# Eight step sums in four PSUM banks instead of four, and one-hots ten steps ahead

## The chip, the cores and the metric

The kernel runs on one core of a Trainium2 chip, as one launch. The metric is the device time of that core in microseconds, the median of the runs shown; lower is better. TensorE is PE in the profile (its weight loads PEld), VectorE is DVE, ScalarE is ACT, GpSimd is POOL and SyncE is SP.

## The reference, cut to what matters

One layer of a graph transformer over 6250 nodes of 256 features and 100,000 edges: two graph convolutions, linear attention beside them, then a mixture of eight experts with the best two for each node. The change touches the sum over edges in the two convolutions:

```python
xw = x @ W
msg = xw[src] * norm[:, None]
out = jax.ops.segment_sum(msg, dst, num_segments=num_nodes)
return out + b
```

`dst` is sorted. `src` is random, so that the rows of the table have to be gathered one edge at a time.

## The kernel before

Everything is fp32. After a preparation of some 100 us the kernel runs the sum of layer 0 (with the keys, values and queries of the attention woven in), a dense part, the sum of layer 1 (with the rest of the attention woven in), then the routing, then the experts. The order is written out by hand: every engine has its own unrolled program, and semaphores tie them.

**The sum.** The 782 tiles of 128 edges and the 49 blocks of 128 nodes give 833 steps (STEPS). A step is one pair of tile and block. Four engines work on it in a chain:

- POOL (`gathers`, L628) fetches one tile at a time, 128 rows of 1 KB, by an indirect DMA into one of 32 places (ROWS). Before it uses a place again it waits for a count `freed` that SP gives.
- SP (`tiles_here`) waits for each tile's transfer and then counts up `here` (L644). For the tile 16 behind it (BEHIND) it waits until the tensor engine's count `summed` has reached the first step of the next tile, and then counts up `freed` (L650). It does both for one tile after the other, in order.
- PE (`step_sum`, L689) multiplies a one-hot matrix, 128 edges by 128 nodes, with the tile: one fp32 matmul of 128x128 by 128x256, which the trace shows as two LDWEIGHTS and two MATMUL records. It writes 256 words of a PSUM bank, half of it, and counts up `summed`. It waits for `here`, and for `added` to reach s - 3: there are four banks (PSB), so step s needs the one of step s - 4 read.
- DVE (`step_add`, L679) waits for `summed` to reach s + 1 and adds the bank's half onto `acc` in SBUF, at an address from a register, and counts up `added`. Every fourth step it also makes the one-hots of four steps (`four_selects`, L657), six steps ahead (AHEAD) in twelve places (SELS), and reads four registers for the next addresses.

**Woven in.** Sixteen steps make a turn, one for each block of nodes. After its step k of a turn an engine does other work (`between`). In layer 0, PE has two transposes at k = 0 (L805), the q, k, v product at k = 3 (L814), for which it waits until ACT has copied the transposes, and the context product at k = 13 (L821, L823), for which it waits for DVE's keys. DVE has three operations at k = 8 (L771, L774, L778), for which it waits for ACT's exponential (L757). In layer 1, DVE makes `qd` at k = 5 (L1043, L1045, L1049) and PE transposes it at k = 8 (L1090), with a wait for it; at k = 11 PE waits for ACT again.

Of the kernel before, what the change touches and what calls it, by code (L numbers as in the profile page):

```python
# [9 lines left out]
ALU = mybir.AluOpType  # L10
# [4 lines left out]
P = 128  # L15
N, D, E = 6250, 256, 100000
# [8 lines left out]
STEPS = NT * SPI  # L25
# [5 lines left out]
PAIRS = -(-NT // 2)  # L31
assert BLOCKS >= 2 * PAIRS + 2
SG = -(-STEPS // P)
ROWS, SELS, FOUR = 32, 12, 4
LOADED = 4
TURN = 16
BEHIND, FREED_AT = 16, 8
# [24 lines left out]
WEIGHTS_AT = 9  # L62
LN_EPS = 1e-5
DEN_MIN = 1e-6
AHEAD = 6
PSB = 4
assert AHEAD >= PSB + 2 and SELS == 3 * FOUR and STEPS <= SG * P - FOUR


def gps_layer(nc, x, src, dst, wqkv, wproj, bproj, gw1, gb1, gw2, gb2, wr, br, wide, vectors, out):  # L70
# [3 lines left out]
    def sem(name):  # L74
        if name not in sems:
            sems[name] = nc.alloc_semaphore(name=name)
        return sems[name]
# [12 lines left out]
    def sb(ctx, name, shape, dt=F32):  # L90
        return ctx.enter_context(nc.sbuf_tensor(name, shape, dt))
# [33 lines left out]
    with whole, nc.allow_non_contiguous_dma("a few columns of one word"):  # L125
# [524 lines left out]
                    sp.sem_inc(sem(f"freed{layer}"), 1)  # L650

        def step_bank(s):
            return step_ps[s % PSB][:, 0:D]

        def four_selects(v, layer, s):

            v.tensor_tensor(sel[:, s % SELS:s % SELS + FOUR, :], iota_n[:, None, :].to_broadcast([P, FOUR, P]),  # L657
                            dloc[:, s:s + FOUR, None].to_broadcast([P, FOUR, P]), ALU.is_equal
                            ).then_inc(sem(f"selected{layer}"), 1)

        def blocks_of(s):

            _, regs = nc.values_load_multi_w_load_instructions(
                words[1:2, s:min(s + LOADED, STEPS), 0], engines=(DVE_ENGINE,), min_val=0, max_val=(BLOCKS - 1) * D,
                skip_runtime_bounds_check_because="a step's tile is one of the step's number or less, by less than the blocks")
            return list(regs)
# [6 lines left out]
            return list(regs)  # L673

        def step_add(v, layer, s, block):
            if s > 0:
                v.wait_ge(sem(f"added{layer}"), s)
            to = acc[:, bass.ds(block, D)]
            v.tensor_tensor(to, to, step_bank(s), ALU.add).wait_op(sem(f"summed{layer}"), s + 1, "sem-ge"  # L679
                                                                   ).then_inc(sem(f"added{layer}"), 1)  # L680

        def step_sum(t, layer, s, here):
            slot = t.snap(here & (ROWS - 1))
            t.to_reg(slot)
            if s < PSB:
                t.wait_ge(sem(f"selected{layer}"), s // FOUR + 1)
            else:
                t.wait_ge(sem(f"added{layer}"), s - PSB + 1)
            t.matmul(step_bank(s), sel[:, s % SELS, :], rows_flat[:, bass.ds(slot * D, D)], start=True, stop=True  # L689
                     ).wait_op(sem(f"here{layer}"), t.to_reg(here), "sem-ge").then_inc(sem(f"summed{layer}"), 1)  # L690

        def vector_steps(v, layer, between):

            blocks = blocks_of(0)
            for s in range(0, 2 * FOUR, FOUR):
                four_selects(v, layer, s)
            for s in range(STEPS):
                if s % LOADED == 1 and s + LOADED - 1 < STEPS:
                    blocks.extend(blocks_of(s + LOADED - 1))
                if s % FOUR == 2 and s + AHEAD < STEPS:  # L700
                    four_selects(v, layer, s + AHEAD)
                step_add(v, layer, s, blocks[s])
                if s < NT * TURN:
                    between(s // TURN, s % TURN)

        def tensor_steps(t, layer, between):

            tiles = tiles_of(0)
            for s in range(STEPS):
                step_sum(t, layer, s, tiles[s])  # L710
                if s % LOADED == 1 and s + LOADED - 1 < STEPS:
                    tiles.extend(tiles_of(s + LOADED - 1))
                if s < NT * TURN:
                    between(s // TURN, s % TURN)
# [8 lines left out]
        with ExitStack() as ph:  # L723
# [10 lines left out]
            step_ps, ps_t, ps_q, ps_v, ps_c, ps_k = bk[0:PSB], bk[PSB], bk[PSB + 1], bk[PSB + 2], bk[PSB + 3], bk[PSB + 3][:, D:]  # L734
# [230 lines left out]
        with ExitStack() as ph:  # L965
# [14 lines left out]
            step_ps, ps_t, ps_d, ps_t2, ps_o = bk[0:PSB], bk[PSB], bk[PSB + 1], bk[PSB + 2], bk[PSB + 3]  # L980
            with nc.Block() as block:
# [53 lines left out]
                def _(v):  # L1035
                    def between(i, k):
# [20 lines left out]
                        if k == TURN - 2:  # L1057
# [5 lines left out]
                            v.wait_ge(sem("a_mix"), i + 1)  # L1063
                            v.tensor_tensor(tile(node, i), tile(node, i), mixb[:, :], ALU.add).then_inc(sem("a_node"), 1)
                    vector_steps(v, 1, between)

                @block.tensor
# [36 lines left out]
        with ExitStack() as ph:  # L1104
# [43 lines left out]
            ge = sb(ph, "ge", [1, FT, NX])  # L1148
# [514 lines left out]
```

## Time and profile before

| | |
|---|---|
| median of 3 runs | 3344.09 us (3339.18 to 3347.60) |
| the profiled execution | 3348.99 us, its span 3346.7 us |
| granted TensorE clock, mean | 0.817 |
| PE, DVE, ACT, POOL busy | 72%, 52%, 19%, 60% of the span |
| sum of layer 0, first to last gather | 100.39 to 1238.40 us of the span |
| sum of layer 1, first to last gather | 1337.10 to 2470.40 us |

Times of instructions count from the start of the span. "Idle before" is the time that an engine did nothing before an instruction, with the one that ended the wait: "SPq L650" is SP's count `freed`, "SPq L644" its count `here`; "issue" and "remote" name no instruction of another engine.

### The profile page before, as it was taken

How to read it: one execution, taken by the hardware profiler on the slowest of the kernel's cores; microseconds unless marked ns; L12 is line 12 of the kernel's file. 1: busy time of each engine (PE TensorE's matmuls, PEld its weight loads, DVE VectorE, ACT ScalarE, POOL GpSimd, SP SyncE). 2: the span in 40 equal slices, each digit the busy share in tenths (PEclk: the TensorE clock that was granted, in tenths of full speed). 3: DMA queues.
4: the chain of work that ended last, by engine and by line, in shares of the span. 5: the costliest groups of instructions: out<-in, count | busy, mean ns of one | idle time of the engine just before them, and what ended most of it. 6: DMA issues, size and time to landing. Idle time of an engine off the chain costs nothing. (4 is left out here: it accounts for less than half of the span.)

```text
span 3346.7 us, 47049 instructions
## 1 busy us (share of the span) xinstructions
PE 2393.5 (72%) x11743; PEld 1816.8 (54%) x11743; DVE 1734.3 (52%) x4351; ACT 620.0 (19%) x1318; POOL 1994.5 (60%) x2107
## 2 busy tenths in 40 slices
PE   3376676666777768366666666666769399999998
PEld 2144444444444446244344444444448199999998
DVE  6144444444444456244444445554556766666665
ACT  1000000000000005000001010101116344444443
POOL 1576766666666653766666666666743055555554
PEclk9777888888777789666767778777779599999999
DMA  6433332333333322444444444444422455555551
GB/s 150 131 94 90 91 92 87 90 91 90 88 90 92 88 77 82 120 137 143 144 137 146 146 136 146 146 147 146 146 73 77 158 180 147 146 147 149 147 147 20
DMA packets 178034, 397.68 MB, mean 119 GB/s; under 512 B 42398, under 2 KB 96575, under 8 KB 169644
## 3 DMA queue, kind: packets, MB, share of 16 engines
q0 software_dynamic: 96800, 233.29, 26.1%
q1 hardware_dynamic: 46516, 99.22, 8.2%
q10 hardware_dynamic: 34552, 63.24, 5.8%
q8 instruction: 69, 1.13, 0.1%
q14 instruction: 97, 0.79, 0.1%
HBM read 323.27 MB, written 75.01 MB: 119 GB/s over the span
## 5 line engine op out<-in xcount | busy, mean ns | idle before, releaser
L628 POOL DMA_INDIRECT rows<-rows_layer,srcs x1564 | 1550.8, 992 | 751.8 <-issue 394.3
L689 PE MATMUL l_bank<-rows,sel 128*128 x3332 | 1207.3, 493 | 639.7 <-issue 246.1
L679 DVE TENSOR_TENSOR acc<-acc,l_bank 128x256 f32 x1666 | 699.5, 420 | 1234.9 <-remote 493.7
L689 PEld LDWEIGHTS l_bank<-rows,sel 128*128 128x128 f32 x3332 | 710.2, 238 | 1012.3 <-issue 468.8
L657 DVE TENSOR_TENSOR sel<-iota_n,dloc 128x512 f32<-128x512 f32 x418 | 286.5, 686 | 20.1 <-issue 20.1
L1574 POOL DMA_INDIRECT out<-ys,g_sum x112 | 180.9, 1615 | 190.0 <-DVE ys L1530 164.8
L1491 ACT ACTIVATE hr<-ffn_bank,vec 128x256 f32<-128x256 f32 x448 | 213.0, 475 | 385.4 <-PE ffn_bank L1432 362.0
L1430 PE MATMUL ffn_bank<-wh,hhi 128*128 128x256 f32 x896 | 257.6, 288 | 0.0
L1430 PE MATMUL ffn_bank<-xh,wh 128*128 128x256 f32 x896 | 252.3, 282 | 2.4 <-DVE xl L1506 2.4
L1432 PE MATMUL ffn_bank<-wh,hlo 128*128 128x256 f32 x896 | 253.1, 282 | 0.0
L1432 PE MATMUL ffn_bank<-xh,wl 128*128 128x256 f32 x896 | 251.9, 281 | 0.0
L1431 PE MATMUL ffn_bank<-xl,wh 128*128 128x256 f32 x896 | 251.9, 281 | 0.0
L1431 PE MATMUL ffn_bank<-wl,hhi 128*128 128x256 f32 x896 | 251.3, 281 | 0.0
L814 PE MATMUL l_bank<-w_qkv,xt 128*128 128x512 f32 (+1 forms) x392 | 179.4, 611 | 42.5 <-issue 28.5
L1515 DVE TENSOR_TENSOR hlo<-hr,hhi 128x256 fp32r<-128x256 f32 x448 | 191.3, 427 | 15.4
L1430 PEld LDWEIGHTS ffn_bank<-xh,wh 128*128 128x128 f32 x896 | 169.8, 189 | 2.8 <-DVE xl L1506 2.8
L1545 POOL DMA_INDIRECT xr<-rows_x,g_row x112 | 133.4, 1191 | 63.3 <-POOL g_row L1541 44.5
L1431 PEld LDWEIGHTS ffn_bank<-wl,hhi 128*128 128x128 f32 x896 | 170.4, 190 | 0.0
L1431 PEld LDWEIGHTS ffn_bank<-xl,wh 128*128 128x128 f32 x896 | 169.9, 190 | 0.0
L1432 PEld LDWEIGHTS ffn_bank<-xh,wl 128*128 128x128 f32 x896 | 169.7, 189 | 0.0
L1430 PEld LDWEIGHTS ffn_bank<-wh,hhi 128*128 128x128 f32 x896 | 168.3, 188 | 0.0
L1432 PEld LDWEIGHTS ffn_bank<-wh,hlo 128*128 128x128 f32 x896 | 167.7, 187 | 0.0
(274 smaller groups left out, 2319.6 us busy)
## 6 DMA issues: line engine op xcount, KB each, us to landing
wh<-w_hi SPq DMA_DIRECT2D x32, 1024.0 KB
wl<-w_lo SPq DMA_DIRECT2D x32, 1024.0 KB
rows<-rows_layer,srcs POOLq DMA_INDIRECT x1564
w_qkv<-wide ACTq DMA_DIRECT2D x49, 335.0 KB
w_hi<-whi ACTq DMA_DIRECT2D x49, 335.0 KB
w_lo<-wlo ACTq DMA_DIRECT2D x49, 335.0 KB
rows_layer<-acc SPq DMA_DIRECT2D x25, 256.0 KB, 2.1
rows_x<-acc SPq DMA_DIRECT2D x7, 910.0 KB
```

The source lines that it names most:

```text
L628: pool.indirect_dma_start(rows[:, (n + 1) % ROWS, :], None, table[layer], bass.IndirectOffsetOnAxis(ap=srcs[:, n:n + 1], axis=0)).then_inc ...
L657: v.tensor_tensor(sel[:, s % SELS:s % SELS + FOUR, :], iota_n[:, None, :].to_broadcast([P, FOUR, P]), dloc[:, s:s + FOUR, None].to_broadca ...
L679: v.tensor_tensor(to, to, step_bank(s), ALU.add).wait_op(sem(f"summed{layer}"), s + 1, "sem-ge").then_inc(sem(f"added{layer}"), 1)
L689: t.matmul(step_bank(s), sel[:, s % SELS, :], rows_flat[:, bass.ds(slot * D, D)], start=True, stop=True).wait_op(sem(f"here{layer}"), t.to ...
L814: ins = t.matmul(to[:, 0:n], xt[:, c, :], w_qkv[:, c, lo:lo + n], start=(c == 0), stop=(c == KC - 1))
L1430: t.matmul(to, a[0], b[0], start=first, stop=False)
L1431: t.matmul(to, a[0], b[1], start=False, stop=False)
L1432: return t.matmul(to, a[1], b[0], start=False, stop=last)
L1491: a.activation(hr[:, m % 4, :], ps_h[m % 4][:, 0:TS], ACT.Gelu, bias=vec[q][:, O_B1 + m:O_B1 + m + 1]).then_inc(sem("e_g"), 1)
L1515: v.tensor_tensor(hl[q][:, m, :], hr[:, m % 4, :], hh[q][:, m, :].bitcast(F32), ALU.subtract).then_inc(sem("e_hs"), 1)
L1545: pool.indirect_dma_start(xr[q][:, h, :], None, rows_x, bass.IndirectOffsetOnAxis(ap=g_row[q][:, h:h + 1], axis=0)).then_inc(sem(f"rows_{q ...
L1574: pool.indirect_dma_start(out, bass.IndirectOffsetOnAxis(ap=g_sum[q][:, h:h + 1], axis=0), ys[q][:, h, :], None, bounds_check=N - 1, oob_i ...
```

## The change

Two following steps share a bank: the even step takes its first 256 words, the odd step the second. With four banks PE may have eight sums written and not yet added. PE waits only ahead of an even step, until both sums of the bank have been added (those of steps s - 8 and s - 7). DVE waits, at the even step, until both sums of the bank are written, then adds one and the other; the odd step waits only for the add before it. The one-hots are made ten steps ahead, in sixteen places, with three groups of four before the first step instead of two.

```diff
--- before.py
+++ after.py
@@ -31,7 +31,7 @@
 PAIRS = -(-NT // 2)
 assert BLOCKS >= 2 * PAIRS + 2
 SG = -(-STEPS // P)
-ROWS, SELS, FOUR = 32, 12, 4
+ROWS, SELS, FOUR = 32, 16, 4
 LOADED = 4
 TURN = 16
 BEHIND, FREED_AT = 16, 8
@@ -62,9 +62,10 @@
 WEIGHTS_AT = 9
 LN_EPS = 1e-5
 DEN_MIN = 1e-6
-AHEAD = 6
 PSB = 4
-assert AHEAD >= PSB + 2 and SELS == 3 * FOUR and STEPS <= SG * P - FOUR
+SUMS = 2 * PSB
+AHEAD = SUMS + 2
+assert AHEAD % FOUR == 2 and SELS >= AHEAD + FOUR + 2 and SELS % FOUR == 0 and STEPS <= SG * P - FOUR
 
 
 def gps_layer(nc, x, src, dst, wqkv, wproj, bproj, gw1, gb1, gw2, gb2, wr, br, wide, vectors, out):
@@ -650,7 +651,7 @@
                     sp.sem_inc(sem(f"freed{layer}"), 1)
 
         def step_bank(s):
-            return step_ps[s % PSB][:, 0:D]
+            return step_ps[s // 2 % PSB][:, s % 2 * D:(s % 2 + 1) * D]
 
         def four_selects(v, layer, s):
 
@@ -673,26 +674,30 @@
             return list(regs)
 
         def step_add(v, layer, s, block):
-            if s > 0:
-                v.wait_ge(sem(f"added{layer}"), s)
             to = acc[:, bass.ds(block, D)]
-            v.tensor_tensor(to, to, step_bank(s), ALU.add).wait_op(sem(f"summed{layer}"), s + 1, "sem-ge"
-                                                                   ).then_inc(sem(f"added{layer}"), 1)
+            if s % 2 == 0:
+                if s > 0:
+                    v.wait_ge(sem(f"added{layer}"), s)
+                v.tensor_tensor(to, to, step_bank(s), ALU.add).wait_op(
+                    sem(f"summed{layer}"), min(s + 2, STEPS), "sem-ge").then_inc(sem(f"added{layer}"), 1)
+            else:
+                v.tensor_tensor(to, to, step_bank(s), ALU.add).wait_op(
+                    sem(f"added{layer}"), s, "sem-ge").then_inc(sem(f"added{layer}"), 1)
 
         def step_sum(t, layer, s, here):
             slot = t.snap(here & (ROWS - 1))
             t.to_reg(slot)
-            if s < PSB:
+            if s < SUMS:
                 t.wait_ge(sem(f"selected{layer}"), s // FOUR + 1)
-            else:
-                t.wait_ge(sem(f"added{layer}"), s - PSB + 1)
+            elif s % 2 == 0:
+                t.wait_ge(sem(f"added{layer}"), s - SUMS + 2)
             t.matmul(step_bank(s), sel[:, s % SELS, :], rows_flat[:, bass.ds(slot * D, D)], start=True, stop=True
                      ).wait_op(sem(f"here{layer}"), t.to_reg(here), "sem-ge").then_inc(sem(f"summed{layer}"), 1)
 
         def vector_steps(v, layer, between):
 
             blocks = blocks_of(0)
-            for s in range(0, 2 * FOUR, FOUR):
+            for s in range(0, AHEAD + 2, FOUR):
                 four_selects(v, layer, s)
             for s in range(STEPS):
                 if s % LOADED == 1 and s + LOADED - 1 < STEPS:
```

## Rows read from the trace of the kernel before

**Rows 1.** The page's costliest groups: the four of the sums.

```profile
L628 POOL DMA_INDIRECT rows<-rows_layer,srcs x1564 | 1550.8, 992 | 751.8 <-issue 394.3
L689 PE MATMUL l_bank<-rows,sel 128*128 x3332 | 1207.3, 493 | 639.7 <-issue 246.1
L679 DVE TENSOR_TENSOR acc<-acc,l_bank 128x256 f32 x1666 | 699.5, 420 | 1234.9 <-remote 493.7
...
L657 DVE TENSOR_TENSOR sel<-iota_n,dloc 128x512 f32<-128x512 f32 x418 | 286.5, 686 | 20.1 <-issue 20.1
```

**Rows 2.** Layer sums and their ends: PE, PEld, DVE, ACT, POOL busy us (count), clock, DMA.

```profile
100.39:1238.40 1138.01, 771.41 (x2486) 484.08 (x2484) 497.77 (x1144) 86.15 (x196) 778.95 (x782) 0.80 0.31 91
1238.40:1267.80 29.40, 21.80 (x70) 13.79 (x70) 19.67 (x46) 0.00 (x0) 0.02 (x1) 0.86 0.02 6
1337.10:2470.40 1133.30, 719.30 (x2192) 477.68 (x2192) 549.85 (x1296) 106.99 (x244) 771.47 (x782) 0.72 0.47 141
2470.40:2497.40 27.00, 18.92 (x62) 11.01 (x62) 17.92 (x41) 0.00 (x0) 0.36 (x1) 0.94 0.02 5
```

**Rows 3.** Who waited for whom, whole span: us in total, times, longest.

```profile
DVE acc L679 <- remote: 493.7, 172, 16.5
...
DVE acc L679 <- PE l_bank L689: 455.5, 366, 4.5
...
POOL rows L628 <- SPq L650: 323.3, 330, 6.9
...
PE l_bank L689 <- DVE acc L679: 165.3, 128, 16.3
```

**Rows 4.** Timeline 594 to 614 us, layer 0: one slow stretch and its end.

```profile
594.17 2.74 PE L814 MATMUL l_bank<-w_qkv,xt 128*128 128x512 f32 x8
...
596.75 1.89 PE L689 MATMUL l_bank<-rows,sel 128*128 x8
...
602.48 0.60 ACT L757 ACTIVATE eq<-l_bank 128x512 f32<-128x512 f32 x1 [9.46 <-remote]
...
603.90 0.42 DVE L679 TENSOR_TENSOR acc<-acc,l_bank 128x256 f32 x1 [7.46 <-issue]
...
604.46 1.22 PE L689 MATMUL l_bank<-rows,sel 128*128 x2 [5.82 <-issue]
606.01 0.42 DVE L679 TENSOR_TENSOR acc<-acc,l_bank 128x256 f32 x1 [1.69 <-PE l_bank L689]
606.28 0.95 POOL L628 DMA_INDIRECT rows<-rows_layer,srcs  x1 [2.33 <-SPq L650]
...
609.95 0.42 DVE L679 TENSOR_TENSOR acc<-acc,l_bank 128x256 f32 x1 [0.35 <-PE l_bank L689]
...
610.29 0.69 DVE L657 TENSOR_TENSOR sel<-iota_n,dloc 128x512 f32<-128x512 f32 x1
...
610.89 1.52 DVE L679 TENSOR_TENSOR acc<-acc,l_bank 128x256 f32 x3
...
613.11 0.42 DVE L679 TENSOR_TENSOR acc<-acc,l_bank 128x256 f32 x1 [0.70 <-DVE acc L679]
```

**Rows 5.** Timeline 145 to 168 us: the end of the first long run of gathers.

```profile
148.06 1.21 PE L689 MATMUL l_bank<-rows,sel 128*128 x2 [4.65 <-issue]
...
157.41 0.96 POOL L628 DMA_INDIRECT rows<-rows_layer,srcs  x1 [0.30 <-issue]
165.01 1.52 DVE L679 TENSOR_TENSOR acc<-acc,l_bank 128x256 f32 x3 [16.49 <-remote]
...
165.28 0.95 POOL L628 DMA_INDIRECT rows<-rows_layer,srcs  x1 [6.92 <-SPq L650]
```

**Rows 6.** Timeline 95 to 106 us: the start of layer 0's sum.

```profile
100.79 1.30 DVE L657 TENSOR_TENSOR sel<-iota_n,dloc 128x512 f32<-128x512 f32 x2 [15.36 <-issue]
...
103.16 1.22 PE L689 MATMUL l_bank<-rows,sel 128*128 x2 [1.97 <-SPq L644]
```

**Rows 7.** Line L1049 (`qd`, layer 1): who waited for it, us and times.

```profile
  PEld l_bank L1090: 20.3, 20
```

## The prediction

> **What bounds the kernel now.** I read the page's groups first, then the busy time of the two stretches that hold the sums, then the waits, and last the timeline of a few single stretches. The groups [rows 1] say where the time can be: the four instructions of a step are the costliest of the kernel, and POOL, PE and DVE each have hundreds of microseconds of idle time in front of them. The stretches [rows 2] say that the gathers span 1138 and 1133 us of the 3347, with 782 gathers in each, one per 1.45 us. No engine is full there: POOL 68%, PE 68 and 63%, DVE 44 and 49%. The change can act only here and in the 29 and 27 us that follow the last gather; the rest does not contain a line of it.
>
> POOL has the highest floor. When it isn't held, it issues a gather every 0.96 + 0.30 = 1.26 us [rows 5]; 781 intervals of that are 984 us. What lies above is 1138.0 - 779.0 - 781 x 0.30 = 124.8 us of pauses in layer 0 and 1133.3 - 771.5 - 234.3 = 127.5 us in layer 1, 252 us in all, and a little for gathers that take longer than 0.96 us (the mean is 0.99). The waits [rows 3] name the cause of the pauses: POOL waits for SP's `freed`. So POOL has filled its 32 places and waits until a tile 31 or so behind has been summed. The sums are late, not the gathers.
>
> Why they are late is the point on which all hangs. DVE waits 456 us for PE by name and 494 us for something that the profile can't name [rows 3]; PE's wait for DVE, that is for a free bank, is only 165 us. The timeline [rows 4] shows such a wait from near. The q, k, v product and four steps of PE are on record from 594.17 to 598.64 us. ACT, which waits for the first, starts at 602.48, and DVE, which waits for the first of the four steps, at 603.90, after 7.46 us idle. PE has used up its four places meanwhile and stands until 604.46, just behind that add. All the time POOL issues a gather each 1.26 us, until its places are full; then it pauses for 2.33 us, in which DVE gets its second sum at 606.01, and SP lets POOL go on at 606.28. The first run of gathers shows the same, larger [rows 5]: PE's step at 148.06 is followed by nothing, POOL issues its last gather at 157.41, and at 165.01 three adds run without a gap. Finished sums arrive slowly while POOL issues without a pause, and in a bunch when it has stopped. What carries this inside the chip the trace doesn't tell. In this kernel POOL stops only when its ring is full.
>
> **The change, part by part.**
>
> More sums ahead. With eight places PE can have eight steps on the way in a slow stretch instead of four, so that up to four more sums arrive in the bunch at its end and SP can free up to four tiles more before POOL's ring is full again. I cost it by pauses. If all are like the one at 606.28, 2.33 - 0.30 = 2.03 us above the usual gap [rows 4], 252 us are 124 pauses, one for 1564 / 124 = 12.6 gathers or 1666 / 124 = 13.4 steps. Four more steps for each would make 17.4 and cut the pauses to 0.77, by 58 us. But PE can't run ahead freely: its own waits in the turn stop it, in layer 0 at k = 3 for ACT and at k = 13 for DVE's step 8, in layer 1 at k = 8 for DVE's step 5, which allows a lead of three, less than four banks already give, and at k = 11 for ACT. I take two thirds of the effect in layer 0 and one third in layer 1, half in all: 29 us. The bounds are nothing (the bunch is no larger, or POOL fills its ring again in the same time) and the whole 252 us.
>
> How the rows of PE are read weighs here. ACT starts 5.6 us behind the recorded end of the product that it waits for [rows 4], so a record of PE can end before its result counts. By its records, though, PE is idle before L689 for want of DVE's add for 165.3 us [rows 3]; taken at their word these go with the deeper ring, and the time would be 3349 - 165 = 3184 us. The Trainium skill's page Perfetto Trace Analysis, section Tensor Engine Instruction (MATMUL, LD_WEIGHTS), says that the end of a matmul is computed from its size and not observed, so that a PE row doesn't prove that the sum is there. The trace agrees, by those 5.6 us. I go by them, and not by PE's idle time: its wait for a bank is then mostly a wait for sums that are late themselves, and more banks don't bring those sooner; that reading is the sum of 29 us above.
>
> The end of each layer. After the last gather 29.4 and 27.0 us pass with no POOL at all; DVE is busy for 19.7 and 17.9 of them [rows 2]. Its own pace, four steps with one group of one-hots, is 613.11 - 609.95 = 3.16 us (the add at 609.95, the group at 610.29, three adds from 610.89, the next at 613.11 [rows 4]), 0.79 us for a step. A deeper ring lets it keep nearer to this: I take 5 us for each layer, 10 in all, between nothing and the idle 9.7 + 9.1 = 19 us.
>
> The waits of DVE and PE. The number of matmuls, adds and counts is unchanged. DVE keeps its two waits for a pair of steps on the sums as one, and odd steps no longer hold the sequencer for `added`. The gap between adds that follow without a stall is (1.52 - 3 x 0.42) / 2 = 0.13 us [rows 4]; if the odd step lost all of it, 833 x 0.13 = 108 us of DVE time would go. DVE is busy less than half of these stretches, so the idle time of [rows 3] hides this; I count nothing on the path, with 108 us as its far bound were DVE the limit, and nothing as the near one.
>
> The cost of pairs. The even add now waits for the odd sum as well. That is the price of the shared bank, and it holds up what stands behind it on DVE: the one-hots, the three operations at k = 8 in layer 0, and `qd` at k = 5 in layer 1. The one-hots are made ten steps ahead, and PE is at most eight ahead: nothing. The others are the rival below; for the likeliest case I count nothing, since PE reaches its wait for the keys five steps later.
>
> The one-hots. As many groups as before, 418 of 0.69 us [rows 1]; four more places cost only SBUF. A third group ahead of the first step moves 0.69 us before the first add of each layer. The first two end at 102.09, PE starts at 103.16 on the first tile and takes 1.22 us on record [rows 6], so the first add can't start before 104.38. The third ends near 102.8: hidden. Without that cover it would cost 1.4 us for both layers.
>
> **The sum.** -29 - 10 = -39 us on the profiled execution's 3349.0: 3310. The median of the runs stands 4.9 us below that execution, so 3305 us, 1.2% faster. A change of 0.3%, 10 us, is about the least that a measurement of this kernel tells from none.
>
> **The rivals.**
>
> *No gain.* Sums reach DVE and SP at the pace that POOL's gathers leave them, however many are on the way. For it: in the first long run PE's step at 148.06 stood on record for 17 us before the adds of 165.01 [rows 5], and POOL's cycle of run and pause could close again at the same 1.45 us. Against it: the bunch at the end of a stall is as long as the ring. Time: 3344, within 10 us. It decides if the pauses are needed to clear the way: then their sum stays at 252 us.
>
> *A large gain.* POOL is never held. For it: PE and DVE are 32 to 56% idle, so nothing but the coupling keeps them. Against it: the waits in the turns, and the slow stretches themselves. With all pauses gone 3344 - 252 - 10 = 3082; by PE's own records 3344 - 165 = 3179. I give weight only to its nearer part, gains over 4%.
>
> *Slower, by the pairs.* In layer 0 the keys at k = 8 stand behind the add of step 8, which now also waits for step 9. Sums late in a slow stretch follow each other by 606.01 - 603.90 = 2.11 us [rows 4], and PE's products at k = 13 wait for the keys. In layer 1 `qd` is behind the add of step 5, and the add of step 4, formerly done by then, now comes with it: 0.55 us (0.42 and the gap of 0.13) in front of `qd`, for which PE waits at k = 8 already now, 20 times with 20.3 us [rows 7]. 49 turns each: at most 49 x 2.11 = 103 us and 49 x 0.55 = 27 us. The loss passes to the end only where PE's wait delays `freed`; at a third of both, 43 us, it outweighs the 39 us of gain, and from there the change is slower. Should the gain be missing as well, half of both gives 3344 + 65 = 3409; one third, the likelier, 3387. The Trainium skill's page PSUM — Partial Sum Buffer, section PSUM bank collisions raise a hardware error, forbids two engines in one bank at a time, even in different columns, so that a kernel can't drop this wait of the pair; no run here shows such a collision.
>
> **How the numbers follow.** Gain by more sums ahead, 0.3 to 4%: 0.46. Gain over 4%: 0.12. No change within 0.3%: 0.22. Slower through the pairs: 0.20. Faster is thus 0.58, same 0.22, slower 0.20. The range goes from 3190 us, a little beyond 4% into the large gain (up to PE's 165 us), to 3375 us, three quarters of the one-third case of the slower rival; about 0.17 is left outside. The likeliest case alone is 3215 to 3333.
>
> **What would show it.** Right: POOL's idle time before L628 falls from 751.8 by some 30 us and the waits for SPq L650 become fewer; the stretches after the last gathers fall to about 24 and 22 us; DVE's L679 shows rows of more adds in a bunch. No gain: the same pause sum, the same 1.45 us for a gather, though PE's waits for DVE's add are gone. Slower: more idle time before L821 in layer 0 and L1090 in layer 1, and more of POOL's time on SPq L650. The prediction is wrong above all if the late sums come from something that the deeper ring itself feeds or relieves: then the pauses move by far more than four steps' worth, either way.

## The result, and the profile after

The changed kernel takes 3335.05 us (median of 5, 3329.50 to 3340.59), the kernel before, beside it, 3344.93 us (median of 5, 3339.18 to 3351.41): a ratio of 0.9964, 95% interval 0.9952 to 0.9976. It is 0.36% faster, 9.9 us, where 39 us were forecast. The profiled execution took 3340.59 us, 8.4 us less than the one of before; its span is 3338.3 us.

The same two kernels were later timed again in two further groups of runs: 0.9959 (0.9945 to 0.9973) and 0.9975 (0.9964 to 0.9986). The gain is small, but it is there.

The page's groups of the changed kernel, with the lines shifted by one to five (the gathers are L629 now, the steps of PE L694, the even and the odd add L681 and L684):

```profile
L629 POOL DMA_INDIRECT rows<-rows_layer,srcs x1564 | 1553.0, 993 | 742.6 <-issue 395.3
L694 PE MATMUL l_bank<-rows,sel 128*128 x3332 | 1040.8, 459 | 215.8 <-DVE acc L684 93.4
...
L681 DVE TENSOR_TENSOR acc<-acc,l_bank 128x256 f32 x834 | 349.1, 419 | 932.9 <-remote 582.6
L684 DVE TENSOR_TENSOR acc<-acc,l_bank 128x256 f32 x832 | 349.9, 421 | 287.6 <-issue 169.5
L819 PE MATMUL l_bank<-w_qkv,xt 128*128 128x512 f32 (+1 forms) x392 | 204.6, 683 | 216.0 <-issue 195.5
L658 DVE TENSOR_TENSOR sel<-iota_n,dloc 128x512 f32<-128x512 f32 x418 | 288.5, 691 | 20.0 <-issue 20.0
```

Against [rows 1], PE's idle time before its steps is a third of what it was, 215.8 us for 639.7, and that of POOL before its gathers has hardly moved, 742.6 for 751.8. DVE's idle time before its adds is 932.9 + 287.6 = 1220.5 us for 1234.9.

The busy time of the two stretches of gathers and of what follows each of them (columns as in [rows 2]):

```profile
104.63:1236.39 1131.76, 705.05 (x2502) 503.90 (x2500) 502.59 (x1150) 86.17 (x196) 775.66 (x782) 0.78 0.32 91
1236.39:1260.93 24.54, 16.13 (x56) 10.33 (x54) 16.98 (x40) 0.00 (x0) 0.01 (x1) 0.93 0.03 6
1331.02:2463.92 1132.90, 683.39 (x2204) 487.69 (x2204) 550.15 (x1298) 107.63 (x244) 777.31 (x782) 0.73 0.47 141
2463.92:2489.47 25.55, 15.87 (x51) 10.37 (x50) 16.97 (x39) 0.00 (x0) 0.00 (x0) 0.87 0.02 6
```

Worked out as in the prediction, POOL's pauses (its idle time above the usual 0.30 us behind each gather) are 1131.76 - 775.66 - 234.3 = 121.8 and 1132.90 - 777.31 - 234.3 = 121.3 us, 243 in all, where they were 252. The ends took 24.54 + 25.55 = 50.1 us, where they took 56.4. So this pair of traces has 9.2 us less in pauses, of which gathers that took longer use up 2.6, and 6.3 us less at the ends. The changed kernel's first gather came 4.2 us later than the other's, which gives part of it back; that leaves the 8.4 us between the spans. The waits:

```profile
DVE acc L681 <- remote: 582.6, 135, 20.8
...
POOL rows L629 <- SPq L651: 314.3, 308, 6.8
...
DVE acc L681 <- PE l_bank L694: 256.2, 129, 9.6
...
PE l_bank L694 <- DVE acc L684: 93.4, 68, 7.3
```

PE waits less for DVE, 93.4 us for 165.3 [rows 3], and POOL waits for SP's `freed` as it did, 314.3 us for 323.3. The rows with `<-remote`, 582.6 us here and 493.7 before, can be named: by the trace's own list of semaphore updates, each of these waits ended at a count of `summed` that is on record more than 1.5 us after the end that PE's last step has on record. They are waits for PE's sums, late ones. The list has gaps: of the 833 counts of `summed` in a layer it holds about 690 and 638 before, 668 and 604 after. So some late sums stand under "issue" too.

The end of the first long run of gathers shows why:

```profile
151.77 0.42 DVE L681 TENSOR_TENSOR acc<-acc,l_bank 128x256 f32 x1 [10.32 <-issue]
...
161.79 0.95 POOL L629 DMA_INDIRECT rows<-rows_layer,srcs  x1 [0.30 <-issue]
169.32 0.42 DVE L681 TENSOR_TENSOR acc<-acc,l_bank 128x256 f32 x1 [15.44 <-remote]
169.41 0.38 ACT L757 ACTIVATE xt<-l_bank 128x256 f32<-128x256 f32 x1 [51.95 <-remote]
169.55 0.95 POOL L629 DMA_INDIRECT rows<-rows_layer,srcs  x1 [6.81 <-SPq L651]
...
169.85 5.49 PE L819 MATMUL l_bank<-w_qkv,xt 128*128 128x512 f32 x8 [26.20 <-issue]
```

POOL pauses here for 6.81 us, as it did for 6.92 [rows 5], and the adds had stood for 15.44 us, as for 16.49. But PE had gone on past its steps and now stands for 26.20 us before the q, k, v product: it waits for ACT, and ACT waits for the transposes, which were late like everything else of PE's. That is where PE's idle time went. Of its products in the turns the kernel before shows

```profile
L814 PE MATMUL l_bank<-w_qkv,xt 128*128 128x512 f32 (+1 forms) x392 | 179.4, 611 | 42.5 <-issue 28.5 <-ACT xt L752 14.0
L821 PE MATMUL l_bank<-qk,vv 128*128 128x128 f32 x196 | 49.3, 341 | 17.8 <-issue 17.6
L1083 PE MATMUL l_bank<-ks_h,qt 128*128 128x8 f32 x196 | 38.9, 308 | 51.1 <-issue 28.8 <-ACT qt L1014 22.3
...
L1090 PE MATMUL l_bank<-ident,w_qkv 128*128 128x128 f32 x98 | 25.6, 352 | 21.2 <-issue 11.6 <-DVE w_qkv L1049 9.5
...
L1076 PE MATMUL l_bank<-ident,qc 128*128 128x128 f32 x98 | 22.7, 321 | 0.0
```

and the changed kernel, beside its L819 above:

```profile
L826 PE MATMUL l_bank<-qk,vv 128*128 128x128 f32 x196 | 56.5, 381 | 78.4 <-issue 41.9 <-DVE qk L783 36.5
L1088 PE MATMUL l_bank<-ks_h,qt 128*128 128x8 f32 x196 | 42.2, 325 | 125.5 <-ACT qt L1019 65.5 <-issue 60.0
...
L1095 PE MATMUL l_bank<-ident,w_qkv 128*128 128x128 f32 x98 | 26.2, 358 | 52.1 <-issue 26.7 <-DVE w_qkv L1054 25.3
L1081 PE MATMUL l_bank<-ident,qc 128*128 128x128 f32 x98 | 25.1, 348 | 141.9 <-ACT qc L1012 92.4 <-issue 49.5
```

The idle time before these five products was 42.5 + 17.8 + 51.1 + 21.2 + 0.0 = 132.6 us and is 216.0 + 78.4 + 125.5 + 52.1 + 141.9 = 613.9 us. With that before the steps it was 772 us and is 830: nothing of PE's waiting went away, it moved from the steps to the products. In the same way the sums grew older as PE got ahead. By the records of the trace, the median time (half of the steps lie below it) from the start of a step's first matmul to the start of its add was 3.1 and 2.8 us in the two layers and is 6.2 and 4.1 us.

The bunches can be counted as well, from the recorded updates of `summed` that follow each other within 0.1 us. Before, the largest bunch is four, the number of sums on the way, and there are 33 and 32 of these in the two layers. In the changed kernel 38 bunches of layer 0 have five to eight counts and 23 of layer 1 have five to eight, and the counts that come alone fell from 511 and 439 to 368 and 379. POOL's pauses did not become much fewer with it: gaps of more than 0.6 us between gathers went from 85 and 97 to 82 and 75, and the remaining ones are longer.

### The profile page after: what moved, and what is told of

Read it like the earlier page. It is cut to its first block and busy times, and to the rows that moved or that the text cites. A ratio compares the mean times of both kernels' runs of the same rounds, so it can differ in the third digit from the quotient of the medians.

```text
span 3338.3 us, 47049 instructions
## 1 busy us (share of the span) xinstructions
PE 2282.6 (68%) x11743; PEld 1842.1 (55%) x11743; DVE 1735.5 (52%) x4351; ACT 620.5 (19%) x1318; POOL 1995.7 (60%) x2107
## 5 line engine op out<-in xcount | busy, mean ns | idle before, releaser
L629 POOL DMA_INDIRECT rows<-rows_layer,srcs x1564 | 1553.0, 993 | 742.6 <-issue 395.3
L694 PE MATMUL l_bank<-rows,sel 128*128 x3332 | 1040.8, 459 | 215.8 <-DVE acc L684 93.4
L694 PEld LDWEIGHTS l_bank<-rows,sel 128*128 128x128 f32 x3332 | 730.6, 232 | 415.3 <-issue 185.9
L681 DVE TENSOR_TENSOR acc<-acc,l_bank 128x256 f32 x834 | 349.1, 419 | 932.9 <-remote 582.6
L684 DVE TENSOR_TENSOR acc<-acc,l_bank 128x256 f32 x832 | 349.9, 421 | 287.6 <-issue 169.5
L819 PE MATMUL l_bank<-w_qkv,xt 128*128 128x512 f32 (+1 forms) x392 | 204.6, 683 | 216.0 <-issue 195.5
L819 PEld LDWEIGHTS l_bank<-w_qkv,xt 128*128 128x128 f32 x392 | 99.8, 265 | 315.9 <-issue 287.9
```

The source lines that it names most:

```text
L629: pool.indirect_dma_start(rows[:, (n + 1) % ROWS, :], None, table[layer], bass.IndirectOffsetOnAxis(ap=srcs[:, n:n + 1], axis=0)).then_inc ...
L819: ins = t.matmul(to[:, 0:n], xt[:, c, :], w_qkv[:, c, lo:lo + n], start=(c == 0), stop=(c == KC - 1))
```

## The experiments

Eighteen kernels ran behind the first measurement, in six groups; those of a group shared the runs of the kernel before, and each ratio is taken within its group. The kernel before had two levels. It took 3344.93 us in the first measurement and 3346.28, 3365.71 and 3346.61 us in three groups, and 3051.74, 3046.46 and 3045.62 us in the other three. Each level held for every kernel and every run of its group. I first took it for a property of the chip, and some expectations below are worded so; the last group disproved it, since the chip with 3051.74 us took 3346.61 us there. What sets the level is not known. I call them the level of 3345 and the level of 3050. The change was designed, profiled and forecast at the level of 3345. The changed kernel was timed only there, in three measurements, and the kernels with two and three banks only at the other level, so that no run parts what the pairs do from what the depth does where sums are late.

**Pairs without more depth, and two kernels with the gathers set free.** This group met the level of 3050 (3051.74 us, 23 runs).

```diff
-PSB = 4
+PSB = 2
```

> Pairs without more depth: two banks hold four sums in pairs. Theory P (late sums come at the pace of the gathers, the number of places hardly matters): within 15 us of the changed kernel, at 3340 to 3355 us. Theory Q (depth is worth something and the pairs cost something that hides it): clearly slower than before, 3370 us or more, and the pair's price is the difference to before.

```diff
-PSB = 4
+PSB = 3
-AHEAD = SUMS + 2
+AHEAD = SUMS + 4
```

> Six sums in three banks. Theory P: within 6 us of the changed kernel (3335). Theory Q: between the two-bank kernel and the changed one, in proportion to the depth.

```diff
-            for n in range(ET):
-                if n >= ROWS:
-                    pool.wait_ge(sem(f"freed{layer}"), n - ROWS + 1)
-                pool.indirect_dma_start(rows[:, (n + 1) % ROWS, :], None, table[layer],
...
+            pool.memset(rows[:, :, :], 0.0).then_inc(sem(f"filled{layer}"), 1)
```

> Leaves out all 1564 gathers: the places are filled with zeros once per layer, SP counts the tiles without a transfer, everything else stays, so the output is not the reference's. Theory P (POOL's gathers make the sums late): no slow stretches; DVE's adds follow PE's records by 1 to 3 us, and each layer's sum takes 833 x 0.8 to 0.9 us plus the turns, 700 to 850 us instead of 1158. Theory R (the engines' own waits in the turns make them late): the layers stay above 1000 us and the slow stretches remain.

```diff
-                    sp.wait_ge(sem(f"summed{layer}"), until[m % FREED_AT])
...
-            t.matmul(step_bank(s), sel[:, s % SELS, :], rows_flat[:, bass.ds(slot * D, D)], start=True, stop=True
+            t.matmul(step_bank(s), sel[:, s % SELS, :], zero[:, :], start=True, stop=True
```

> The sums read a constant tile of zeros instead of the gathered rows, and SP frees a place as soon as the transfer 16 tiles on has landed, so that POOL is never held; the gathers and their number stay, the output is not the reference's. Theory P: POOL issues at 1.26 us all through, 985 us per layer, and as it never pauses the sums crawl all that time: many are still to do when the gathers end. Theory R: the layer ends shortly after the gathers, at 1010 to 1050 us, as the sums keep up.

Measured: two_banks 3057.37 us, 1.0023 (1.0014 to 1.0033); three_banks 3057.94 us, 1.0028 (1.0016 to 1.0039); free_gathers 3057.26 us; no_gathers 2441.26 us. At this level the sums of two_banks are never late: each of its 2 x 833 counts of `summed` is on record 0.013 to 0.015 us behind the recorded end of its step, and the list of updates has no gaps. Its two stretches of gathers:

```profile
100.90:1104.46 1003.56, 787.65 (x2542) 489.18 (x2540) 518.03 (x1183) 86.04 (x196) 765.48 (x782) 0.85 0.36 103
...
1181.40:2190.56 1009.16, 728.76 (x2244) 465.04 (x2244) 566.07 (x1330) 108.06 (x244) 771.21 (x782) 0.79 0.53 159
```

POOL's pauses are 1003.56 - 765.48 - 234.3 = 3.8 us and 3.7 us, where they were 125 and 128, and POOL is two to three gathers ahead of PE where it was 27. The pace is the floor of 1.26 us and a few hundredths. So depth can't be told from no depth here, and the forecasts of both theories for two_banks and three_banks (3335 us and above), which were made for the other level, stay untested. These three, and one_pass and before_half_ring of a later group, have five different edits and all lie 0.2 to 0.3% above the kernel before, free_gathers too, in which nothing of the sums holds POOL. I can't lay that to the pairs.

**The change again, with fewer counts, and with something behind each gather.** Level of 3345 (3346.28 us, 23 runs). The first two have no edit.

> The kernel before, for its profile on this chip. Theory C: with 3052 us no wait of DVE on 'remote' above 50 us in all, POOL's pauses below 50 us in all, 8 us from the last gather to the last add; with 3345 us the rows of the first profile.

> The changed kernel as it is, on the chip of this group. The first group ran where the kernel before took 3052 us instead of 3345, with POOL at its floor and no late sums. Theory C (the late sums belong to the circumstances of the first measurement, and where they are missing the change only costs): where the kernel before takes about 3052 us, this one is 0.2 to 0.4% slower, as the two- and three-bank kernels were; where it takes about 3345, 0.3 to 0.4% faster. Theory D (four pairs gain everywhere): faster in both.

```diff
-                     ).wait_op(sem(f"here{layer}"), t.to_reg(here), "sem-ge").then_inc(sem(f"summed{layer}"), 1)
+                           ).wait_op(sem(f"here{layer}"), t.to_reg(here), "sem-ge")
+            if s % 2 == 1:
+                ins.then_inc(sem(f"summed{layer}"), 2)
```

> The changed kernel with `summed` counted once per pair, up by two at the odd step. Theory P1 (late sums because each count of PE is slow to arrive): where the sums are late, half as many counts gives more than 1% over the changed kernel. Theory P2 (the path is held for a time, however many counts wait): same as the changed kernel within 0.3%. Where the sums aren't late: within 0.3% of the changed kernel, or slower by the half pair that SP waits longer.

```diff
+                pool.memset(idle[:, n:n + 1], 0.0)
```

> The changed kernel with one memset of one word per partition on POOL behind each gather, so that the gathers are issued at a slower and even pace. Theory P (the unbroken run of gathers makes the sums late): where the sums are late, they are late less, and the time falls although POOL does more. Where they aren't late: slower by 1564 times what the memset adds to POOL's interval, 100 to 250 us if that is 60 to 160 ns.

Measured: before_again 3344.16 us; after_again 3334.55 us, 0.9959 (0.9945 to 0.9973); one_count 3337.42 us, 0.9977 (0.9968 to 0.9987); paced 3343.61 us, 0.9997 (0.9986 to 1.0007). Stretches and ends of before_again and then of after_again:

```profile
104.32:1236.50 1132.18, 769.03 (x2482) 481.34 (x2480) 496.09 (x1142) 86.16 (x196) 775.03 (x782) 0.80 0.32 91
1236.50:1266.90 30.40, 23.25 (x76) 14.44 (x74) 20.54 (x48) 0.00 (x0) 0.01 (x1) 0.88 0.02 5
1335.79:2466.05 1130.26, 711.97 (x2192) 469.39 (x2192) 549.39 (x1295) 106.43 (x244) 768.13 (x782) 0.73 0.48 142
2466.05:2493.47 27.42, 19.09 (x63) 10.95 (x62) 18.33 (x42) 0.00 (x0) 0.00 (x0) 0.94 0.02 5
```

```profile
105.40:1237.42 1132.02, 712.32 (x2498) 504.13 (x2496) 501.89 (x1150) 86.02 (x196) 770.46 (x782) 0.78 0.32 91
1237.42:1261.64 24.22, 16.12 (x60) 9.84 (x58) 17.34 (x41) 0.00 (x0) 0.41 (x1) 0.97 0.02 7
1331.01:2462.52 1131.51, 666.00 (x2200) 478.83 (x2200) 549.79 (x1296) 107.61 (x244) 771.60 (x782) 0.74 0.48 141
2462.52:2489.26 26.74, 17.26 (x54) 11.42 (x54) 17.82 (x41) 0.00 (x0) 0.00 (x0) 0.87 0.02 6
```

The pauses are 250.7 and 252.9 us: the 9 us of the first pair of traces don't repeat, and can't be laid to the change. The ends are 57.8 and 51.0 us: the 6 us repeat. Some 3 to 5 us of the gain of 9 to 12 stay unplaced. Half as many counts by PE bring no time over the changed kernel (3337.42 us for 3334.55; its pauses are 237 us), so their number isn't what makes sums late. Paced didn't pace: POOL shows

```profile
593.32 0.96 POOL L630 DMA_INDIRECT rows<-rows_layer,srcs  x1 [0.19 <-issue]
594.27 0.12 POOL L633 MEMSET idle<- 128x1 f32 x1
594.58 0.96 POOL L630 DMA_INDIRECT rows<-rows_layer,srcs  x1 [0.19 <-issue]
```

A gather still comes each 1.26 us, the memset lies in the gap of 0.30 us. The kernel is 9 us slower than the changed kernel in the same group, and why is not known. It decides nothing on pacing.

**Real pacing, and rests.** This group met the level of 3050 (3046.46 us, 13 runs), where no sum is late. The edits of the first two are those of the kernels of their names; the others:

> The changed kernel without gathers, once more: its places are filled once with zeros and SP counts without a transfer; its output is not the reference's. It took 2441 us on the chip on which the kernel before took 3052 us, with sums of 698 and 709 us. Read only beside a kernel before of about 3345 us, where sums are late; at 3052 us it is a repetition. Theory 1 (sums are late because POOL issues gathers without a pause): 2441 us within 1%, no late sums, layers of about 700 us; all of the difference between the two chips is the gathers' doing. Rival (PE, DVE and SP signal late on that chip whatever POOL does): the late sums stay, and layers take over 850 us, 2750 us or more in all.

> The changed kernel with the same gathers, but the sums read a tile of zeros, and SP counts freed without waiting for summed, so that POOL is never held by a late sum; its output is not the reference's. On the chip with 3052 us it took 3057 us. Where the kernel before takes about 3345 us, theory 1 (unbroken gathers hold the sums back): POOL issues all 782 gathers at 1.26 to 1.29 us each, the sums fall ever further behind, DVE's last add comes 100 us or more after the last gather, and a layer is no shorter than before (1150 us), or hardly. Rival (POOL's waits for freed are the cost, and sums are late only within the lag that the ring allows): last adds within 35 us of the last gather, layers of 1040 us, and 3100 us in all.

```diff
+                pool.memset(idle[:, n % 2, :], 0.0).then_inc(sem(f"idle{layer}"), 1)
+                pool.wait_ge(sem(f"idle{layer}"), n + 1)
```

> The changed kernel, with a memset of 256 columns on POOL behind each gather (some 0.3 us) and a wait for it, so that gathers come every 1.40 to 1.45 us and never closer. Where the kernel before takes about 3345 us: theory 1 (what holds sums back is POOL issuing without a gap of some size): the sums come on time, the lag falls from 25 gathers to under 10, the tails from 25 to under 12 us, POOL's waits for freed go, and the time is 782 x 1.43 us for a layer, 3300 to 3330 us. Rival (what matters is the number of gathers on the way, or POOL must stand fully still): lag and waits as before, and the pace added: 3345 to 3400 us. Where the kernel before takes 3052 us both expect 782 x 2 x 0.15 = 235 us more, 3290 us.

```diff
+                if n % 8 == 7:
+                    pool.memset(idle[:, :], 0.0).then_inc(sem(f"idle{layer}"), 1)
+                    pool.wait_ge(sem(f"idle{layer}"), n // 8 + 1)
```

> The changed kernel, with one memset of 1600 columns on POOL behind each eighth gather (some 1.3 us) and a wait for it: POOL stands still with its gathers at a time of its own, before its ring is full. Where the kernel before takes about 3345 us: theory 1, with the pauses as what clears the way: late sums arrive in these pauses, the lag falls under 16, the tails under 15 us, and the pauses for freed (145 us for a layer in all) are replaced by 97 x 1.3 = 126 us: 3290 to 3335 us. Rival (a pause of 1.3 us is too short, sums need POOL's earlier gathers to drain): the waits for freed shrink by less than the rests add, 3340 to 3450 us. Where the kernel before takes 3052 us both expect about 2 x 110 us more, 3270 us.

Measured: no_gathers_2 2440.98 us; free_gathers_2 3051.04 us, 1.0018 (1.0008 to 1.0027); paced_wide 3516.61 us; rest_of_eight 3327.55 us. The last two show only that time added to POOL's gathers is time added to the kernel. The memset and its wait put 0.33 + 0.27 us behind each gather, 1.56 us from one to the next, more than I had reckoned (1.40 to 1.45), and the time grew by 470 us, not by 235. None of the four says anything on late sums. Whether pacing would help at the level of 3345 wasn't tried.

**Is it the gathers, and is it the ring.** Level of 3345 (3365.71 us, 17 runs). after_3 has no edit, no_gathers_3 the edit of no_gathers.

> The changed kernel itself. Where the kernel before takes about 3345 us: a repetition, 3335 us, ratio 0.996. Where it takes about 3050 us, no sum is late and PE never waits long for a bank, so that more depth buys nothing: theory 1 (the pairs delay the even add by one step and so `freed` and what stands behind it) gives a ratio of 1.002 to 1.003, as the kernels with two and three banks of pairs had there (1.0023 and 1.0028). Rival (depth makes up for the pairs): 0.998 to 1.000.

```diff
-ROWS, SELS, FOUR = 32, 16, 4
+ROWS, SELS, FOUR = 16, 16, 4
-BEHIND, FREED_AT = 16, 8
+BEHIND, FREED_AT = 8, 8
```

> The changed kernel with 16 places for gathered tiles instead of 32, and SP freeing the tile 8 behind instead of 16. Where the kernel before takes about 3345 us: theory 1 (POOL must stop for late sums to come, and it stops when its ring is full) says that POOL stops about as often again and each stop is shorter: lag near 12 instead of 25, tails 13 instead of 25 us, pace within 2% of 1.448 us, 3290 to 3350 us. Rival (what a stop costs is its own length, and there are twice as many): pace 1.6 us or more, 3550 us. Where the kernel before takes about 3050 us, the lag is 2 to 3 gathers and SP frees 8 behind: no change, 3055 to 3065 us.

> The changed kernel without gathers (places filled once with zeros, SP counts without a transfer; its output is not the reference's). It took 2441 us on both chips on which the kernel before takes 3050 us. Where the kernel before takes about 3345 us: theory 1 (late sums come from the gathers) 2441 us within 1% and no late sum; rival (PE, DVE and SP signal late there whatever POOL does) 2700 us or more.

Measured: after_3 3356.39 us, 0.9975 (0.9964 to 0.9986); half_ring 3326.07 us, 0.9886 (0.9869 to 0.9902); no_gathers_3 2441.57 us. Without gathers the level of 3345 is gone: the same 2441 us as at the other level. No wait is put down to "remote" before the adds any more. The adds of no_gathers_3:

```profile
L680 DVE TENSOR_TENSOR acc<-acc,l_bank 128x256 f32 x832 | 350.0, 421 | 253.6 <-DVE acc L677 211.9
L677 DVE TENSOR_TENSOR acc<-acc,l_bank 128x256 f32 x834 | 348.7, 418 | 85.0 <-PE l_bank L690 38.6
```

So sums are late only where gathers run (with the gathers their transfers are gone too, and the two weren't parted). The short ring tells more. Stretches and ends of after_3 and then of half_ring:

```profile
103.75:1242.63 1138.88, 719.62 (x2502) 511.76 (x2500) 503.58 (x1150) 86.02 (x196) 771.31 (x782) 0.78 0.31 91
1242.63:1268.05 25.42, 15.74 (x55) 10.38 (x54) 16.97 (x40) 0.00 (x0) 0.00 (x0) 0.93 0.03 7
1336.93:2477.06 1140.13, 672.16 (x2196) 477.46 (x2196) 548.47 (x1293) 107.86 (x244) 773.76 (x782) 0.74 0.48 140
2477.06:2505.94 28.88, 17.58 (x58) 11.10 (x58) 19.16 (x44) 0.00 (x0) 0.00 (x0) 0.85 0.02 5
```

```profile
100.07:1238.23 1138.16, 744.00 (x2527) 538.82 (x2525) 511.17 (x1168) 86.01 (x196) 774.02 (x782) 0.77 0.31 91
1238.23:1253.38 15.15, 10.23 (x30) 7.09 (x30) 9.46 (x23) 0.00 (x0) 0.00 (x1) 0.73 0.04 10
1323.20:2463.54 1140.34, 693.00 (x2234) 486.90 (x2235) 558.73 (x1319) 108.08 (x244) 771.37 (x782) 0.75 0.47 140
2463.54:2474.44 10.90, 5.84 (x21) 3.22 (x20) 7.86 (x18) 0.00 (x0) 0.00 (x0) 1.00 0.06 13
```

The gathers take the same 1138 and 1140 us with 32 places and with 16. The pauses are 265.4 and 264.5 us. And they are the same pauses: after_3's and then half_ring's wait for `freed` are

```profile
POOL rows L629 <- SPq L651: 320.8, 310, 6.8
```

```profile
POOL rows L629 <- SPq L651: 328.5, 306, 3.3
```

The longest is shorter, their number and sum are not. The rival had expected twice as many of the same length, a pace of 1.6 us or more. Theory 1 had the pace, the ends and the time. All of the gain lies at the ends: 54.3 us became 26.1, 28 us of the 30 by which half_ring beats after_3. POOL is some 26 tiles ahead of PE with 32 places and some 10 with 16, and what it is ahead by at its last gather has still to be summed.

**The short ring without the change, and one matmul record for a step.** The first pair met the level of 3050 (3045.62 us, 22 runs).

```diff
-ROWS, SELS, FOUR = 32, 12, 4
+ROWS, SELS, FOUR = 16, 12, 4
-BEHIND, FREED_AT = 16, 8
+BEHIND, FREED_AT = 8, 8
```

> The kernel before (four sums in four banks), with 16 places for gathered tiles instead of 32, and SP freeing the tile 8 behind. Where the kernel before takes 3345 to 3366 us: theory 1 (late sums come at a fixed rate while gathers run; only the tiles that POOL is ahead at the end cost time) gives the same 1.456 us per gather, tails of 13 to 16 us instead of 27 to 30, and 0.990 to 0.992 of the kernel before, so that the shorter ring gains three times what the change does. Rival (the short ring needs the eight sums on the way): 1.000 or more. Where the kernel before takes 3050 us, POOL is 2 to 3 gathers ahead: 0.999 to 1.001.

```diff
+            rows_high = rows_flat.bitcast(BF16).rearrange("p (n t) -> p t n", t=2)[:, 1, :]
-            sel = sb(ph, "sel0", [P, SELS, P])
+            sel = sb(ph, "sel0", [P, SELS, P], BF16)
-            t.matmul(step_bank(s), sel[:, s % SELS, :], rows_flat[:, bass.ds(slot * D, D)], start=True, stop=True
+            t.matmul(step_bank(s), sel[:, s % SELS, :], rows_high[:, bass.ds(slot * D, D)], start=True, stop=True
```

> The changed kernel with one-hots in bf16 and the tile read as the upper halves of its fp32 words, so that a step is one matmul record of PE instead of two; the gathered rows are cut to bf16 in the sums. Where the kernel before takes 3345 to 3366 us: theory 1 (while gathers run each matmul record of PE costs some 0.7 us until its result counts, two for a step, 1.4 us a step) halves the steps' share: sums keep up, the pace falls under 1.33 us per gather, and 3060 to 3170 us. Rival (the rate is per step, count or bank, not per record): 1.44 to 1.46 us per gather, 3300 to 3350 us. Where the kernel before takes 3050 us both expect 3040 to 3060 us, the gathers' own pace.

Measured: before_half_ring 3052.56 us, 1.0022 (1.0013 to 1.0031), a loss a little beyond what both sides allowed; one_pass 3053.13 us, 1.0026 (1.0016 to 1.0036). The last run has both edits on the kernel before, and met the level of 3345 (3346.61 us, 7 runs).

> The kernel before with 16 places instead of 32 (freed 8 behind), and with one-hots in bf16 and the tile read as the upper halves of its words, one matmul record a step; the gathered rows are cut to bf16 in the sums. Where the kernel before takes 3345 to 3366 us: theory 1 (0.7 us for each matmul record of PE while gathers run, two a step in the kernel before) brings the pace under 1.33 us per gather and the time to 3060 to 3170 us. Rival (the rate is not PE's records): 1.44 to 1.46 us per gather, and then the tails, 13 to 16 us with the short ring or 27 to 30 without its gain, say whether the short ring gains without the change: 3310 to 3330 us or 3340 to 3360 us. Where the kernel before takes 3050 us: 3045 to 3060 us by both.

Measured: 3297.17 us, 0.9860 (0.9841 to 0.9880), outside all three forecasts.

```profile
103.43:1232.65 1129.22, 542.74 (x1713) 294.46 (x1711) 511.27 (x1180) 86.02 (x196) 772.66 (x782) 0.62 0.32 91
1232.65:1238.68 6.03, 3.04 (x11) 1.72 (x10) 3.88 (x10) 0.00 (x0) 0.00 (x1) 0.50 0.08 24
1310.02:2434.23 1124.21, 442.88 (x1412) 218.05 (x1412) 558.45 (x1323) 107.17 (x244) 760.55 (x782) 0.52 0.48 142
2434.23:2442.75 8.52, 3.45 (x10) 0.94 (x9) 6.08 (x15) 0.00 (x0) 0.00 (x0) 0.50 0.06 16
```

With half of PE's records for the steps the pauses are 122.3 + 129.4 = 251.7 us, the 252 of the kernel before, at 1.44 us per gather. The theory of 0.7 us for each record falls, and the rival's pace of 1.44 to 1.46 us holds. The ends fell to 14.6 us, some 42 us less than the 56 and 58 us of the kernel before in other groups, of the 49 us gained here; the two edits can't be parted in that, but it shows that short ends don't need eight sums on the way. What the short ring alone does to the kernel before, where sums are late, wasn't timed.

## Why the prediction was wrong

**The step that failed: "More sums ahead ... 29 us".** It took the pauses to be set by how many sums a bunch holds: four more steps in each bunch, so fewer pauses, 58 us less of 252, of which it took half. Its first half came true, the bunches grew from four counts to five to eight. Its second half failed: the pauses measured 252.3 and 250.7 us before and 243.1 and 252.9 us after, a gain of 9 us in one pair of traces and a loss of 2 in the other. Fewer sums arrive singly between the bunches, and the pace stays at 1.45 us for a gather. A ring of 16 tiles on the changed kernel (264.5 us for 265.4), half as many counts (237) and half of PE's records together with the short ring (251.7) left the pauses near where they were. The prediction divided 252 us into 124 equal pauses, one for 12.6 gathers, as if four more places lengthened that cycle by four steps; the measured gaps of over 0.6 us are 182 before and 157 after, 176 and 166 in the second pair, and what they lost in number they gained in length. As far as these runs go, late sums come at a pace that more places don't change, and places only make what waits in them older. [rows 5] could have warned: a wait of 17 us isn't hidden by eight places of 1.4 us each any more than by four.

**The rival that held is the one named *No gain*.** The sum of the pauses stays, the pace is 1.45 us as before, and PE's wait for the add fell, though it isn't gone, as the rival had said. Its argument against itself, that the bunch is as long as the ring, was true and decided nothing. It put the time at 3344 within 10; 3335.05 is within that, and 6 to 7 of the 9.9 us by which it is under the kernel before are the ends, which the rival left out.

**The ends: two thirds in size, and in kind right in part.** 10 us forecast; 6.3 us in the first pair of traces and 6.9 us in the second. Not all of it is what was forecast, DVE nearer to its own pace. DVE's busy time in the ends fell by 3.6 and 3.7 us, as fewer sums are left when the gathers stop (PE had 33 and 32 steps to start after the last gather was issued, and has 27 and 26); its idle time there fell by 2.7 and 3.2 us. Where the ring was cut to 16 tiles 13 and 11 steps are left and the ends fell by 28 us.

**How PE's rows are read: right in the outcome, not in the reason.** To take the 165 us of waiting for the add at their word would have given 3184 us; PE's idle time moved from its steps to its products (772 us in all before, 830 after) and no time came of it. By the Trainium skill's page Perfetto Trace Analysis, section Tensor Engine Instruction (MATMUL, LD_WEIGHTS), the end of a matmul is computed and not observed. The prediction took the 5.6 us of [rows 4] for a sign of this, but the traces don't bear that out: at the level of 3050 the counts of `summed` stand 0.013 to 0.015 us behind the computed ends, all of them. At the level of 3345 the four steps that [rows 4] has from 596.75 end by 598.64 on record, and the next counts of `summed` on record are four from 605.99 to 606.11. The gap is thus lateness, of the product or of its count, and not an end that was computed too early as a rule.

**The pairs: no cost seen, as forecast.** PE's idle time before the products that wait for the keys and for `qd` rose, 17.8 to 78.4 us and 21.2 to 52.1 us, as the rival *Slower by the pairs* had it, but POOL's wait for `freed` did not. PE also reaches these products earlier now, so that a part of these waits need not be loss at all. A kernel with pairs and no more depth would price them, and none was timed at this level. The one-hots cost nothing: DVE's idle time before them is 20.0 us, where it was 20.1.

**The range** of 3190 to 3375 us held the time, and 3215 to 3333 for the likeliest case just missed it.

**What stays open** is what carries the lateness. It needs gathers running, and it needs a condition that sets the level of 3345 and can be absent on the same chip. Of what was varied at that level, none removes it: eight sums on the way for four, 16 places for 32, half as many counts of PE, half of PE's records for a step. Whether POOL's spacing matters there, or the gathers' transfers and not their issue, wasn't tried.

## What to carry to other kernels

Before you deepen a buffer, ask whether the wait in front of it is a rate or a jitter. If what is upstream of it is full as well, and the same pause follows each run, it is likely a rate: a deeper buffer moves the idle time to the next wait, and here over 400 us of PE's idle time moved for a gain of 10. Halving the buffer tests it: here the pauses stayed at 265 us with half the ring. A buffer that is always full has a price: what is in it at the end has still to be worked off, so with late sums the changed kernel with 16 places beats that with 32 by 0.9% (3326 us against 3356). It isn't a free gain: where sums came on time, the same cut made the kernel before 0.22% slower (1.0013 to 1.0031), and the cut on the changed kernel wasn't timed there, nor the cut alone on the kernel before where sums are late.

## What the runs showed of the hardware

The same kernel had two times, 9 to 10% apart (3345 to 3366 and 3046 to 3052 us), each stable within its group, one chip showing both. The whole of it lay in the stretches with indirect gathers and their ends: they take 2327.7 us in the kernel before at the one level and 2027.0 in two_banks at the other, 300.7 us apart, and the spans of these traces are 300.8 us apart. Without gathers the kernel took 2441 us in groups of both levels.

At the level of 3345, SP's own counts were slow too. By the trace's records between 200 and 1230 us of after_3, 704 counts of `here` took 75 us in all, 73 of them 0.6 to 1.4 us each, the median 0.017 us; in two_banks, at the level of 3050, none of 741 took more than 0.017 us. The kernel before shows what it does to the ring: between 152 and 160 us, in the stretch of [rows 5], SP counts `freed` at 152.34, 154.44, 156.55 and 159.35, one tile per 2.1 us or more, most of these counts and those of `here` between them taking 0.7 us, while POOL issues a gather per 1.26 us. Late were thus not only PE's sums but also what SP counts by itself.
